# Gated RWKV and int8 feed-forward layer: gate and up inputs quantised as 16-bit whole numbers where they are read, by three engines, and VectorE's block loop written out

## What is computed

```python
def _act_fake_quant(x, clip_factor):
    scale = jax.nn.sigmoid(clip_factor) * jnp.max(jnp.abs(x)) / QMAX
    return jnp.clip(_ste_round(x / scale), -QMAX - 1.0, QMAX) * scale
...
xq = _act_fake_quant(x, clip_x[0])
gate = jnp.einsum('bsh,ih->bsi', xq, _weight_fake_quant(w_gate))
up = jnp.einsum('bsh,ih->bsi', xq, _weight_fake_quant(w_up))
h = _act_fake_quant(jax.nn.silu(gate) * up, clip_down[0])
return jnp.einsum('bsi,hi->bsh', h, _weight_fake_quant(w_down))
...
x = x + jnp.tanh(g_ffn[0]) * _L0_ffn_ref(_layernorm(x, axis=-1), ...)
```

## Time and profile before

| | us |
|---|---|
| median of 3 runs | 218.35 (218.22 to 220.37) |
| the profiled execution | 217.56 |
| its span | 215.6 |
| busy in the span: TensorE | 169.9 |
| VectorE | 170.5 |
| ScalarE | 155.7 |
| POOL | 137.4 |
| mean granted TensorE clock | 0.93 |

### The profile page before, as it was taken

One profiled execution on the slowest core, in us unless ns is written; L12 is line 12 of the kernel. 1 busy time (PEld: TensorE's weight loads), 2 busy tenths in 40 slices (PEclk: granted clock), 3 DMA queues, 4 the chain that ended last, 5 costly groups with the idle time before them and its releaser, 6 DMA issues.

```text
span 215.6 us, 3369 instructions
## 1 busy us (share of the span) xinstructions
PE 169.9 (79%) x1121; PEld 122.7 (57%) x1126; DVE 170.5 (79%) x345; ACT 155.7 (72%) x235; POOL 137.4 (64%) x157
## 2 busy tenths in 40 slices
PE   4599977959899999972078888599799924989950
PEld 4456527959899999962056553234243403756620
DVE  0769495537657689997689679997999998999992
ACT  3459698573996996996479978578798844899400
POOL 3364223469399999884688807749887750039991
PEclk9969999999999999999556999999999995899995
DMA  3999999999999996300000000000000000004458
GB/s 98 341 371 348 348 319 292 287 292 298 289 320 252 267 243 177 101 0 2 0 0 0 0 3 2 0 0 0 3 0 0 0 0 0 3 0 146 167 195 273
DMA packets 43327, 29.30 MB, mean 136 GB/s; under 512 B 2224, under 2 KB 43056, under 8 KB 43312
## 3 DMA queue, kind: packets, MB, share of 16 engines
q1 hardware_dynamic: 43168, 28.84, 46.7%
q10 hardware_dynamic: 144, 0.26, 0.3%
HBM read 24.65 MB, written 4.46 MB: 135 GB/s over the span
## 4 chain that ended last, share of the span: by engine, by line
PE 36%; DVE 25%; ACT 14%; DMA 9%; issue 7%; POOL 3%; SPq 1%; DVEq 1%; ACTq 0%
PE ps L909 10%; PE ps L1002 9%; PE ps L1035 8%; DMA hidden<-lag_w 6%; PE ps L893 5%; DVE hidden L799 4%; DMA hidden<-in_ctx 3%; ACT hidden L504 3%; DVE h_space L856 2%; DVE hidden L817 2%; PE ps L940 2%; DVE h_peaks L828 2%; ACT silu_out L623 2%; ACT hidden L575 2%; DVE bn L679 2%
## 5 line engine op out<-in xcount | busy, mean ns | idle before, releaser
L909 PE MATMUL ps<-hidden 128*128 128x128 f32 (+1 forms) x512 | 58.7, 276 | 6.3 <-DMA hidden<-lag_w 3.0
L909 PEld LDWEIGHTS ps<-hidden 128*128 128x128 f32 x512 | 57.8, 192 | 7.6 <-issue 3.3
L397 POOL TENSOR_TENSOR x_all<-x_all,silu_out 128x512 f32<-128x512 f32 x16 | 24.3, 1526 | 8.2 <-DVE silu_out L715 8.2
L828 DVE TENSOR_REDUCE h_peaks<-hidden (+2 forms) x24 | 26.0, 1123 | 2.0 <-POOL hidden L440 1.3
L1035 PE MATMUL ps<-wdT,z_t 128*128 128x256 bf16 (+1 forms) x192 | 25.0, 285 | 2.9 <-ACT z_t L637 2.9
L706 DVE SCALAR_TENSOR_TENSOR h_space<-z_t,ps 128x256 f32<-128x256 f32 x32 | 18.9, 595 | 8.9 <-PE ps L909 8.7
L637 ACT ACTIVATE z_t<-h_space 128x1024 bf16<-128x1024 int8 (+3 forms) x12 | 20.1, 1754 | 6.8 <-DVE h_space L856 6.8
L1035 PEld LDWEIGHTS ps<-wdT,z_t 128*128 128x128 bf16 (+1 forms) x192 | 17.0, 101 | 10.8 <-issue 4.8
L623 ACT ACTIVATE silu_out<-ps,mix_scale 128x1024 f32<-128x1024 f32 (+1 forms) x18 | 18.3, 1019 | 5.8 <-PE ps L1002 3.4
L933 PE MATMUL ps<-ident,hidden 128*128 128x128 f32 x64 | 11.6, 342 | 12.6 <-POOL hidden L421 11.1
L453 POOL TENSOR_TENSOR x_all<-x_all,z_t 128x512 f32<-128x512 f32 x6 | 10.7, 1802 | 15.5 <-DVE z_t L874 15.5
(11 more groups left out here) (105 smaller groups left out, 357.2 us busy)
## 6 DMA issues: line engine op xcount, KB each, us to landing
hidden<-lag_w SPq DMA_DIRECT2D x26, 512.0 KB, 7.3
x_all<-in_x SPq DMA_DIRECT2D x8, 512.0 KB, 8.8
hidden<-in_ctx SPq DMA_DIRECT2D x8, 512.0 KB, 9.0
out<-x_all SPq DMA_DIRECT2D x16, 256.0 KB, 2.4
xq<-in_L_ffn_w_down SPq DMA_DIRECT2D x1, 704.0 KB, 5.9
xq<-in_L_ffn_w_gate SPq DMA_DIRECT2D x1, 640.0 KB, 6.9
h_space<-in_L_ffn_w_up SPq DMA_DIRECT2D x1, 640.0 KB, 6.0
lag_w<-up_out ACTq DMA_DIRECT2D x1, 255.0 KB, 7.2
```

Source lines behind the costliest of these rows:

```text
L397: nc.gpsimd.tensor_tensor(xs, xs, mixed[:, m % 2, :, :].rearrange("p c b -> p b c"), ALU.add).then_inc(s["x1_done"], 1)
L828: nc.vector.tensor_reduce(h_peaks[:, bass.ds(KA * b + k, 1)], hidden[:, bass.ds(b * HB + k * BT, cols)], AX.X, ALU.max, apply_absolute_val ...
L909: last = nc.tensor.matmul(ps[:, j % BANKS, c * 2 * SEQS:end * 2 * SEQS], lag_tile(j)[:, c, :], ekp[:, (j * CK + c) * 2 * SEQS:(j * CK + en ...
```

## The change

Six things. VectorE, ScalarE and POOL each write whole numbers as int16 in the bytes of the bf16 tile that TensorE will read (`x_int`): VectorE the halves 0, 2, 3, ScalarE the half 1, POOL the halves 4 to 7. int16 does not saturate at 127, so a second instruction is needed on every half: VectorE casts it in place to bf16 with min and max. `x8` is gone. POOL's quantisations all stand ahead of its first product, and wait for VectorE's two parts of half 0 and ScalarE's half 1, over whose fp32 numbers they write. POOL's casts between blocks are gone. VectorE's loop over blocks 1 to 3 is written out.

```diff
+        X_BY_DVE, X_BY_ACT, X_BY_POOL = [0, 2, 3], [1], [4, 5, 6, 7]
+
+        def x_int(n):
+            return whole_x(n // 2)[:, n % 2, :, :].bitcast(I16)
...
-            def cast_x(b):
-                for n in (2 * b, 2 * b + 1):
-                    pool.wait_ge(s["x8_done"], n + 1)
-                    nc.gpsimd.tensor_copy(whole_x(b)[:, n % 2, :, :], x8[:, n, :, :]).then_inc(s["xq_cast"], 1)
+            def quantise_x(n):
+
+                pool.wait_ge(s["x_int_own"], 2)
+                pool.wait_ge(s["x_int_act"], 1)
+                nc.gpsimd.tensor_scalar(x_int(n), x_normed(n), S["inv_x"], 1.0, ALU.mult, ALU.mult).then_inc(s["x_int_pool"], 1)
...
-            cast_x(1)
+            for n in X_BY_POOL:
+                quantise_x(n)
             for b in range(BLOCKS):
                 for i in range(EVEN):
                     multiply(b, i)
-                if b + 2 < BLOCKS:
-                    cast_x(b + 2)
...
-            cast_first()
+            act.wait_ge(s["inv_x_done"], 1)
+            act.wait_ge(s["z_kept"], 2)
+            for n in X_BY_ACT:
+                nc.scalar.activation(x_int(n), x_normed(n), ACT.Copy, scale=S["inv_x"]).then_inc(s["x_int_act"], 1)
...
-            def quantise_x(n):
+            def quantise_x(n, h=None):
                 dve.wait_ge(s["z_kept"], n + 1)
-                nc.vector.tensor_scalar(x8[:, n, :, :], z_t[:, :, n * 512:(n + 1) * 512], S["inv_x"], None,
-                                        ALU.mult).then_inc(s["x8_done"], 1)
...
+                nc.vector.tensor_scalar(x_int(n)[:, halves, :], x_normed(n)[:, halves, :], S["inv_x"], None, ALU.mult) \
+                    .then_inc(s["x_int_own"], 1)
...
+                nc.vector.tensor_scalar(whole_x(n // 2)[:, n % 2, halves, :], x_int(n)[:, halves, :], QMAX, -QMAX - 1.0,
+                                        ALU.min, ALU.max).then_inc(s["xq_done"], 1)
...
-            for n in range(2, GROUPS):
+            for n in (2, 3):
                 quantise_x(n)
+                cast_x(n)
...
+                if b == 0:
+                    peak(b, 1)
+                    for n in X_BY_POOL:
+                        cast_x(n)
+                    peak(b, 0)
...
-            hidden_block(0, True)
-            with dve.Fori(1, BLOCKS) as b:
-                hidden_block(b, False)
```

More of the change, by code:

```diff
@@ L28 @@
 I8 = mybir.dt.int8
+I16 = mybir.dt.int16
 P = 128
@@ L795, in _, with cast_x @@
             nc.vector.sem_inc(s["h_odd"], ODD)
-            def quantise_x(n):
+            nc.vector.sem_inc(s["inv_x_done"], 1)
+            def quantise_x(n, h=None):
                 dve.wait_ge(s["z_kept"], n + 1)
-                nc.vector.tensor_scalar(x8[:, n, :, :], z_t[:, :, n * 512:(n + 1) * 512], S["inv_x"], None,
-                                        ALU.mult).then_inc(s["x8_done"], 1)
-            dve.wait_ge(s["z_kept"], 1)
+                halves = slice(0, CH) if h is None else slice(h, h + 1)
+                nc.vector.tensor_scalar(x_int(n)[:, halves, :], x_normed(n)[:, halves, :], S["inv_x"], None, ALU.mult) \
+                    .then_inc(s["x_int_own"], 1)
+            def cast_x(n, h=None):
+                if n in X_BY_DVE:
+                    dve.wait_ge(s["x_int_own"], X_BY_DVE.index(n) + 1 + (1 if n > 0 or h == 1 else 0))
+                elif n in X_BY_ACT:
+                    dve.wait_ge(s["x_int_act"], X_BY_ACT.index(n) + 1)
+                else:
+                    dve.wait_ge(s["x_int_pool"], X_BY_POOL.index(n) + 1)
+                halves = slice(0, CH) if h is None else slice(h, h + 1)
+                nc.vector.tensor_scalar(whole_x(n // 2)[:, n % 2, halves, :], x_int(n)[:, halves, :], QMAX, -QMAX - 1.0,
+                                        ALU.min, ALU.max).then_inc(s["xq_done"], 1)
             for h in range(CH):
-                nc.vector.tensor_scalar(x8[:, 0, h, :], z_t[:, h, 0:512], S["inv_x"], None, ALU.mult) \
-                    .then_inc(s[("x8_half", "x8_done")[h]], 1)
-            quantise_x(1)
+                quantise_x(0, h)
+                cast_x(0, h)
+            cast_x(1)
             nc.vector.tensor_scalar(mix_scale[:, :, :], w_scale[:, :, :], S["s_x"], None, ALU.mult).then_inc(s["scale_x"], 1)
-            dve.wait_ge(s["scale_x"], 1)
-            for n in range(2, GROUPS):
+            for n in (2, 3):
                 quantise_x(n)
+                cast_x(n)
             def multiply(b, k):
@@ L817, in multiply @@
                 nc.vector.scalar_tensor_tensor(
-                    hidden[:, bass.ds(b * HB + k * BT, cols)],
+                    hidden[:, b * HB + k * BT:b * HB + k * BT + cols],
                     ps[:, 6:8, :].rearrange("p a n -> p (a n)")[:, 0:cols],
@@ L827, in peak @@
                     dve.wait_ge(s["h_even"], EVEN * b + k // 2 + 1)
-                nc.vector.tensor_reduce(h_peaks[:, bass.ds(KA * b + k, 1)], hidden[:, bass.ds(b * HB + k * BT, cols)],
+                nc.vector.tensor_reduce(h_peaks[:, KA * b + k:KA * b + k + 1], hidden[:, b * HB + k * BT:b * HB + k * BT + cols],
                                         AX.X, ALU.max, apply_absolute_value=True).then_inc(s["hpeak_done"], 1)
-            def hidden_block(b, first):
-                peak(b - 1, 4) if not first else None
-                multiply(b, 1)
-                peak(b, 0)
-                peak(b, 1)
+            for b in range(BLOCKS):
+                if b > 0:
+                    peak(b - 1, 4)
+                else:
+                    dve.wait_ge(s["scale_x"], 1)
+                multiply(b, 1)
+                if b == 0:
[3 more added lines that the diff above has]
+                    peak(b, 0)
+                else:
+                    peak(b, 0)
+                    peak(b, 1)
                 multiply(b, 3)
```

19 lines of the change are left out of this document (5 added, 14 removed).

## The result

| | before | changed |
|---|---|---|
| median us (20 runs each) | 218.65 (217.42 to 220.53) | 220.01 (218.81 to 222.20) |
| ratio | 1 | 1.0051 (95%: 1.0030 to 1.0072) |
| profiled execution | 217.56 | 220.44 |
| its span | 215.6 | 219.0 |

One execution of the changed kernel, the 222.20, was in a slower state and is left out of the ratio. The change made the kernel about 0.5%, 1.1 us by the ratio, slower. The forecast was +1.2 us on the median of 218.35, thus 219.5. The size was right. Several of the terms that it was made of were not, and the rest of this document is about that.

A forecast was written before the change was run, and what follows sets the result against it. VectorE, full from block 0's first multiply on, was taken to set the stage's end together with that multiply's start. Terms +1.5 +1.6 -1.2 -0.7 = +1.2 on the 218.35 median gave 219.5 us, range 218.0 to 221.0.

The forecast's parts named there:

- rival A: VectorE's 16-bit casts do not exclude POOL, so block 0's first multiply starts near 135.0; 215.4 us, chance 0.17.
- B: Rival: POOL's quantisation is slow (1.5 to 1.68 us) or the cast runs at 0.75; 222 us, chance 0.20.
- T: Start of VectorE's first multiply in block 0, put between 138.0 and 140.2, taken as 139.1: +1.5 us.
- Four late casts: VectorE's casts of POOL's halves between block 0's first peaks, with POOL idle there: 0.48 each less overlap, +1.6 us.
- rival C: TensorE's clock falls in its stall before block 0's first multiply; +1 on +2.3, 221.6 us, chance 0.08.
- No loop: Writing out VectorE's blocks 1 to 3 could give back 1.3 us; half counted, -0.7, bounds 0 and -1.3.
- (1): Sign: VectorE's whole-half 16-bit cast takes 0.48 when POOL sleeps, otherwise ends 0.3 after POOL's instruction.
- (2): Sign: POOL's four quantisations take about 1.1 us granted, 1.3 to 1.5 with turns.
- (5): Sign: block 1's peak 0 on VectorE no longer waits for POOL.
- (3): Sign: the first multiply starts between 138 and 140.2, with TensorE waiting for it 2.7 to 4.9 us.
- (4): Sign: four casts stand between two peaks in block 0, 1.6 us together.
- (6): Sign: blocks 1 to 3 take 9.6 to 9.9 us each.

The follow-up runs named there:

- e1: Changed kernel, but POOL's second product of block 0 waits until VectorE's nine casts are done; 216.61 us, ratio to before 0.9896.
- e5: Changed kernel with VectorE's loop over blocks 1 to 3 put back; 220.67 us, ratio to before 1.009.
- e8: Changed kernel run again unaltered, with a second look at its trace; 221.22 us, ratio to before 1.0114.
- e2: Changed kernel with TensorE's gate product k = 5 of block 0 done six times over; 218.25 us, ratio to before 0.9958.
- e4: Kernel before with VectorE's loop over blocks 1 to 3 written out, nothing else; 219.13 us, ratio to before 1.0002.
- e7: Kernel before with TensorE's gate product k = 3 of block 0 done three times over; 218.18 us, ratio to before 0.9976.
- e10: Second run of the changed kernel with POOL's second product of block 0 waiting for VectorE's nine casts; 215.88 us, ratio to before 0.9889.
- e9: Changed kernel, POOL's first two products waiting for VectorE's casts, two POOL quantisations moved to block 1, their casts to block 2; 214.82 us, ratio to before 0.9826.

## Why the prediction was right, and where it was not

The total was +1.2 us and the mechanism named (the two engines exclude each other, so the work is moved but costs its turns) is what the runs show. By its own steps:

1. **The casts exclude POOL; a turn ends 0.28 after POOL's instruction, a quantisation's 0.55.** Right: 0.28, 0.28, 0.54. This refutes rival A. By the Trainium skill's rule ("SBUF — State Buffer", SBUF: two separate sides) the one who comes first holds the port pair for its whole instruction; the trace agrees for the 16-bit casts, with 2.45 us beside a product against 0.41 alone.
2. **Prices.** Cast 0.48 whole, 0.35 half: measured 0.41 and 0.29. POOL's quantisation 1.13 alone and 0.99 after its turn: measured 1.11, and 0.98 from quantise 2's end at 133.22 to 134.20. This refutes B. ScalarE's 1.06: measured 1.15. The first halves end at s + 1.8 as worked out.
3. **T at 139.1, +1.5 us. Wrong, by 3.3 us.** It came out at -1.85. The failed step is the sentence that sets "POOL's before them: four quantisations, 3.96, and its first product 2.21", with half of the second product on top. I let POOL go first at every turn. Two of VectorE's six instructions needed no turn, cast 1 because POOL's first had not been let in, quantise 2 because mix_scale is so short that VectorE's next starts 0.05 us before POOL's. I had seen such a tie, but only for the last cast. POOL's quantisations then lasted until 136.98 and its product found the last cast in front of it. Without the two products the same sum gives s + 7.76, and 7.67 was measured. mix_scale ended at s + 3.06 against my 4.1, and the first SiLU began at s + 3.15 against 4.8.
4. **Four late casts, +1.6. Wrong: +3.48.** Their own price was nearly right (1.42 in e1). The clause "POOL is idle there" failed. It followed from the wrong T: with both products earlier POOL would have been idle. e1 shows that the missing 2.0 us are POOL's second product and nothing else.
5. **The clock, rival C, 0.08.** It belonged in the sum. C was about the stall in which TensorE waits for multiply 1, which was only 1.02 us; the clock fell behind the one ahead of up k = 5, 3.6 us long, in all three traces of the changed kernel's order (this one, e5, e8), and by e2 the fall cost 1.5 to 2.7 us of the stage. I took a stall of some 4 us to cost nothing from one row, the stage's end of before, where TensorE was idle from 174.2 and the clock still 1.00 at 177 to 178. e4 shows a fall behind a stall of 2.22, and e7's stage end the same idle as before's, from 174.8 on, with the clock already down at 176 to 177:

```profile
176.00:177.00 1.00, 0.00 (x0) 0.00 (x0) 1.00 (x2) 0.00 (x0) 1.00 (x1) 0.82 0.00 0
```

6. **The wait of 1.26 in block 1 goes, -1.2.** From multiply 1 of block 1 to that of block 2 it is 0.88 less in the changed kernel, 1.16 in e1. Nearly right.
7. **No loop, -0.7. Wrong: about 0.** Block 2 is 0.31 shorter and block 3 not at all, and e5 gets the same total with the loop in. The bound of 0 held.
8. **2.0 us around the span, and the rest unchanged.** Neither is a term of the sum, both are premises: the time outside the span fell by about 0.4, and what comes behind the stage is some 0.3 longer.

The terms sum to -1.85 + 3.48 + 1.16 - 0.88 - 0.31 + 0.01 = +1.61 in the profiled executions. That this is near +1.2 is in large part luck. With the clock at 1.00 the same queues give a stage of 50.57 us (e2), 0.1 above before: what the forecast's own terms stand for came to +0.1, not +1.2, and the fall of the clock, which the sum did not have, brought the other 1.5. Item 3 and item 4 hide each other in part, since the second product is in both: half of it was counted in T, and it was paid in full at the late casts. The first product, 2.21 in T, cost VectorE nothing.

The main case's range, 218.0 to 221.0, held the time. Of the signs that I named, (1), (2) and (5) came true, though POOL's four quantisations took 1.28 to 1.67 us, not 1.3 to 1.5. (3) did not (TensorE waited 1.02 us, not 2.7 to 4.9), nor did (4) (3.45, not 1.6), and (6) only in part (10.3, 9.7 and 10.0). One sign of being wrong came true as well: counted from s, the first multiply starts where 135.7 was in the profile before, and I had named a start before 136 as the mark of A. A is refuted all the same, so that mark was badly chosen: fewer turns moved the multiply nearly as far as no exclusion would have.

What stays open: how often the clock falls in the kernel before, and with it how much of the 0.5% is that. With TensorE kept at work in both, nothing is left between the kernels that these runs can tell: ratios 0.9958 (0.9924 to 0.9993) for e2 and 0.9976 (0.9941 to 1.0012) for e7, stages of 50.57 and 50.50 us.

## What to carry to other kernels

When two engines exclude each other on a form of instruction, what matters is not how much work each has but who stands in whose way at which moment. List both queues with their start times, and look for the few instructions on the critical engine that meet a long one of the other. Then make the other wait with a semaphore: here one added wait turned +0.5% into -1.0% and -1.1% (e1, e10) with the same work, and a second one, with two of POOL's instructions moved into block 1, into -1.7% (e9). And if one instruction is taken out of such a pair of queues, ask what moves up into its place.

## What the runs showed of the hardware that was not expected

- An instruction of 12 elements on VectorE took 1.02 us, against 0.23 before, and ended 0.03 us after POOL's quantisation. The SiLU that waits for it started at 132.67, 0.36 after TensorE's product.
- A 16-bit cast in place with min and max takes 0.41 us for 128x1024 and 0.34 from start to start, against 0.75 for an fp32 to int8 one.
- TensorE's granted clock fell to 0.50 behind stalls of 3.6 us (three times in three) and, with a stall of 2.2 us, in e4 but not in the profile before. With a harmless product repeated in the stall it stayed at 1.00 (e2). The same in the kernel before (e7) shows nothing more, since the profile before had no fall there either.
- The order of turns was the same in all seven traces with the changed kernel's queues up to there (multiply 1 at s + 7.60 to 7.70), although it hangs on 0.05 us.
